# A four-layer network on one core: the mixer stage as one run over both batch pairs, and conditioning units that scan backward over the forward scan's result

## The chip, the cores and the metric

The kernel runs on one core of one Trainium2 chip. Its time is the device time of that core in microseconds (us), here the median of three runs. A core has TensorE for matrix products (PE; its weight loads are listed as PEld), VectorE (DVE), ScalarE (ACT), GpSimd (POOL), and SyncE (SP), which issues the DMAs. PE, DVE, ACT and POOL each take their instructions in a fixed order and wait for each other on semaphores.

## The reference

Four batches of 256 tokens by 256 channels pass through four layers. Ahead of each layer stands a conditioning step, and `x = x + layer(condition(x, f, f, w, u, emb))`, where `f` is the same side input each time:

```python
tf = sigmoid(sum(time_emb, -1))[:, None, None]
decay = exp(-exp(w))[None, :] * (0.5 + 0.5 * tf[:, :, 0])
ek = exp(minimum(k, 30)); ekv = ek * v                 # k = v = f
nf, df = scan(a * decay + ekv, b * decay + ek)         # over 256 tokens, forward
nb, db = the same, reverse=True
euk = exp(minimum(u + k, 30))
num = nf + nb - ekv + euk * v
den = df + db - ek + euk
out = sigmoid(r) * (num / maximum(den, 1e-8)) * (0.8 + 0.2 * tf)   # r = x
```

The layers are a Mamba2 mixer (32 heads of 64, state 128, conv of 4 taps, SiLU gate, RMS norm, output projection), a mixture of 16 experts (4 picked) with a shared one, latent attention with 16 heads, and grouped-query attention with a mixture of 8 experts.

## The kernel before, in words

Channels lie on the 128 partitions. The four batches are two **pairs**; one pair is 2 batches x 256 tokens = 512 columns (`TOK`), and a tensor of 256 channels by one pair is 1024 columns (`UNIT`). The stages follow one another with a barrier of all engines between them: `stage_condition`, `stage_mixer`, `stage_moe` (first mixture), `stage_latent_attention`, `stage_gqa`, `stage_moe` (second).

A **conditioning unit** (`CondUnit`) makes the factor `m` = num / den x scale of one conditioning step for one pair. It depends on `f` alone, not on `x`, so the kernel makes the units of later layers beside the matrix work of earlier stages. `CondUnit.vector` returns a list of 26 small steps for DVE: `add_u` (2), four scans (`den`, `den_b`, `num`, `num_b`; 2 steps each, and each step is two scans of 256 columns), `combine` (2, adds the backward denominator), `add_own` (2), `bound` (2), `invert` (8 reciprocals of 128 columns) and `factor` (2). `take(steps, n)` issues the next n of them. POOL makes the numerator in four operations on 1024 columns (`pool_numerator`), and ACT makes one exponential (`scalar`). `stage_condition` makes both pairs' units for the mixer, one after the other, and `make_h(pair)` ends each: `h = (tanh(x/2) + 1) * m`. `stage_mixer` carries the two units of the first mixture, the first mixture those of latent attention, and latent attention those of the last layer.

**The mixer** goes over the pairs (`for i in range(PAIRS)`), and for each pair over 16 tiles of 128 inner channels, two heads a tile, in `STEPS = 16 + 4` steps. At step s each engine works on several tiles at once:

- PE: `x_like(s+2)` and `gate_like(s)` project (4 matmul instructions of 512 columns each, since float32 goes in two passes), `spread_cum` (two per step) writes each head's running decay sums to PSUM, `turn_x(s-1)` transposes, `project_out(s-4)` projects out, `mix(s-3)` multiplies values with decays (16 instructions, one head on output partitions 0 to 63, then the other on 64 to 127).
- ACT: `begin_conv`, `exp_decay` (two per step, 4 exponentials each), `tanh_conv`, `tanh_gate`, `square_g`.
- POOL: `scale_decay` twice (128x768) and `add_square` once (128x512), and at four steps one operation of `pool_numerator`.
- DVE: `taps` (3 instructions of the convolution, read from PSUM), `gated(s-3)` (y and g), `silu_x`, `take_x(s-1)`, `silu_gate(s)`, and then `take(cond, 2)`, two steps of the unit. That last place in a step is called the **slot** below.

Before its first tile each pair has a **prologue**: the projections for dt, B and C, the softplus (`softplus_cum`), the running sums and their split in three bfloat16 parts (`cum_parts`), their transposes (`turn_cum`, `row_cols`), and the products of B and C (`key_query`, taken by DVE as `scores`). B and C go through the same PSUM bank, convolution and SiLU as the tiles. After its last tile each pair has an **end**: the sum of squares over channels (one matmul), its inverse root on ACT (a logarithm and an exponential), and `add_to_x`. Semaphore counts set the order; nothing is scheduled by a planner.

The memory of the prologue is shared: `z`, `soft`, `dt` and `cum` lie in the buffer of `gate`, and `root` in that of `y`, so that a pair's prologue has to wait for the pair before. PSUM has eight banks, all in use.

Of the kernel before, what the change touches and what calls it, by code (L numbers as in the profile page):

```python
# [91 lines left out]
class Net:  # L92


    def __init__(self, nc, stack, dram):
# [23 lines left out]
        self.dcol = sb("dcol", [P, 4 * KT * BATCH])  # L119
        self.scol = sb("scol", [P, BATCH])  # L120
# [44 lines left out]
class CondUnit:  # L165


    VECTOR_LINKS = 7 * KT

    def __init__(self, net, c, sems):  # L170
        self.net, self.c = net, c
        (self.u_ready, self.euk_ready, self.scans_done, self.own_ready,
         self.factor_made, self.num_steps) = sems

    def pool_numerator(self, pair, turn):

        net, nc = self.net, self.net.nc
        pool = nc.gpsimd
        both = slice(pair * UNIT, (pair + 1) * UNIT)

        def own():
            pool.wait_ge(self.euk_ready, turn + 1)
            pool.tensor_tensor(net.euk[:], net.euk[:], net.e[:, both], ALU.subtract) \  # L183
                .then_inc(self.own_ready, 1)

        def own_times_f():
            pool.wait_ge(self.own_ready, turn + 1)
            pool.wait_ge(self.num_steps, 3 * turn)
            pool.tensor_tensor(net.own_f[:], net.euk[:], net.f[:, both], ALU.mult) \
                .then_inc(self.num_steps, 1)  # L190

        def add_backward():
            pool.wait_ge(self.scans_done, turn + 1)
            pool.tensor_tensor(net.num[:], net.num[:], net.num_b[:], ALU.add) \
                .then_inc(self.num_steps, 1)

        def add_own():
            pool.wait_ge(self.num_steps, 3 * turn + 2)
            pool.tensor_tensor(net.num[:], net.num[:], net.own_f[:], ALU.add) \
                .then_inc(self.num_steps, 1)  # L200

        return own, own_times_f, add_backward, add_own
# [7 lines left out]
    def vector(self, link, pair, turn):  # L210
# [4 lines left out]

        def columns(k):
# [5 lines left out]
        done = [None] * KT  # L222

        def on(k, op):
            done[k] = link.mark(op)

        def after(k):
            if done[k] is not None:
                v.wait_ge(*done[k])
# [9 lines left out]
        def scan(out, x, reverse=False):  # L239
            order = slice(None, None, -1) if reverse else slice(None)  # L240

# [33 lines left out]
        def invert(part):  # L275
# [4 lines left out]
            if part == INVERT_PARTS - 1:  # L280
                link(op)
# [157 lines left out]

# [1855 lines left out]
```

## Time and profile before

| | |
|---|---|
| median of 3 runs | 1437.3 us (1430.36 to 1439.8) |
| the profiled execution | 1430.53 us, its span 1428.7 us |
| granted TensorE clock, mean | 0.952 of full speed |
| conditioning stage | 0 to 62.5 us |
| mixer stage | 62.5 to 459.4 us |
| first mixture | 459.4 to 739.5 us |
| latent attention | 739.5 to 939.5 us |

The stage bounds are read from the timeline (the first instruction of a stage after the barrier). A busy share is the time in which an engine has an instruction under way. That time includes waits inside an instruction, for example for a port of the memory. The time ahead of an instruction in which its engine stood idle stands in square brackets at the end of its row, with the instruction that ended the wait.

### The profile page before, as it was taken

The page shows a single profiled execution, that of the slowest core. Times are in us where ns is not written, and L with a number is a line of the kernel's source. Part 1 is how long each engine was busy: PE and PEld are TensorE (multiplying, and loading weights), DVE is VectorE, ACT ScalarE, POOL GpSimd, SP SyncE. Part 2 cuts the span into 40 slices and gives each one's busy share as a digit, 9 for nine tenths or more (in the row PEclk, how much of TensorE's full clock was granted, in tenths as well). Part 3 has the DMA queues.
Part 4 walks back from the last instruction along what each step waited for, and adds up shares of the span by engine and source line. Part 5 has one row for each costly group of instructions (what it writes and reads, how often), then busy time and mean ns, then how long its engine had stood idle before and what let it go on. Part 6 is the DMA issues. An engine that isn't in the chain of part 4 may idle for free. (4 is left out here: it accounts for less than half of the span.)

```text
span 1428.7 us, 14494 instructions
## 1 busy us (share of the span) xinstructions
PE 1208.1 (85%) x4614; PEld 642.9 (45%) x4614; DVE 863.4 (60%) x1306; ACT 585.7 (41%) x1732; POOL 512.9 (36%) x499
## 2 busy tenths in 40 slices
PE   0277998688996899999987998978799887987998
PEld 0033454243443444444444655633585346834443
DVE  8789986699993563265236839639750596414222
ACT  1154554354544222222225545647572585700110
POOL 5634576045754110020002827627551375500000
PEclk9999999999998799999997999989899998997999
DMA  6000000000021300000020000030000000000000
GB/s 256 22 1 1 1 1 1 1 0 1 1 83 70 129 1 0 1 0 0 34 111 37 1 0 1 2 140 0 1 2 0 0 1 1 2 0 8 0 0 30
DMA packets 4730, 33.53 MB, mean 23 GB/s; under 512 B 528, under 2 KB 912, under 8 KB 2768
## 3 DMA queue, kind: packets, MB, share of 16 engines
q1 hardware_dynamic: 4656, 32.61, 5.8%
q8 instruction: 38, 0.62, 0.2%
q14 instruction: 36, 0.29, 0.1%
HBM read 31.56 MB, written 1.05 MB: 23 GB/s over the span
## 5 line engine op out<-in xcount | busy, mean ns | idle before, releaser
L780 POOL TENSOR_TENSOR decays<-decays,scores 128x768 f32<-128x768 f32 x64 | 123.3, 1929 | 173.9 <-ACT decays L716 173.6
L1371 POOL TENSOR_TENSOR prob_latent<-prob_latent,inverse_latent 128x128 f32<-128x128 f32 (+1 forms) x128 | 78.6, 637 | 187.1 <-DVE inverse_latent L1361 186.9
L1962 POOL TENSOR_TENSOR euk<-m,weights 128x256 f32<-128x256 f32 x80 | 91.1, 1157 | 91.3 <-DVE m L1983 79.7
L542 PE MATMUL pg<-h,weights 128*128 128x512 f32 (+1 forms) x136 | 66.3, 610 | 65.2 <-PEq L328 62.7
L1067 PE MATMUL ph<-h,weights 128*128 128x512 f32 x256 | 116.8, 601 | 0.0
L542 PE MATMUL px<-h,weights 128*128 128x512 f32 x136 | 73.2, 664 | 32.9 <-DVE conv L852 32.8
L716 ACT ACTIVATE decays<-pcum,neg_cum 128x256 f32<-128x256 f32 (+1 forms) x256 | 87.9, 450 | 12.4 <-PE pcum L595 12.4
L1211 DVE TENSOR_TENSOR mid<-up,ph 128x512 f32<-128x512 f32 x44 | 30.2, 686 | 96.8 <-ACT up L1124 96.8
L1124 ACT ACTIVATE up<-ph 128x512 f32<-128x512 f32 x44 | 26.3, 597 | 140.1 <-PE ph L1067 140.1
L1371 POOL TENSOR_TENSOR prob_gqa<-prob_gqa,inverse_gqa 128x128 f32<-128x128 f32 (+1 forms) x128 | 62.2, 508 | 57.8 <-DVE inverse_gqa L1361 56.1
L852 DVE SCALAR_TENSOR_TENSOR conv<-px,pp,conv 128x510 f32<-128x510 f32 (+2 forms) x102 | 75.2, 737 | 11.8 <-ACT conv L681 9.3
L688 ACT ACTIVATE tanh_x<-conv 128x512 f32<-128x512 f32 x36 | 22.5, 630 | 144.0 <-DVE conv L852 144.0
L1067 PEld LDWEIGHTS ph<-h,weights 128*128 128x128 f32 x256 | 49.4, 193 | 62.2 <-issue 62.1
L183 POOL TENSOR_TENSOR euk<-euk,e 128x1024 f32<-128x1024 f32 x8 | 21.2, 2652 | 150.8 <-ACT euk L208 150.8
L622 PE MATMUL py<-decays,x_tok 128*64 128x128 f32 (+1 forms) x512 | 71.2, 332 | 0.0
L636 PE MATMUL pout<-g,weights 128*128 128x512 f32 x128 | 64.0, 624 | 6.3 <-DVE g L908 6.3
L622 PEld LDWEIGHTS py<-decays,x_tok 128*64 128x64 f32 x512 | 51.9, 137 | 36.1 <-issue 24.5
L1238 DVE TENSOR_TENSOR mid<-act_out,ph 128x512 f32<-128x512 f32 x22 | 15.1, 688 | 81.4 <-ACT act_out L1118 81.4
L1118 ACT ACTIVATE act_out<-ph 128x512 f32<-128x512 f32 x26 | 15.5, 597 | 112.9 <-PE ph L1067 112.8
L542 PEld LDWEIGHTS pg<-h,weights 128*128 128x128 f32 (+1 forms) x136 | 23.4, 191 | 85.0 <-issue 84.6
L1085 PE MATMUL pmoe<-hidden,weights 128*128 128x512 f32 x128 | 60.2, 591 | 0.0
L1067 PE MATMUL ph<-h,moe_rest 128*128 128x512 f32 x128 | 57.5, 592 | 0.0
(317 smaller groups left out, 2955.7 us busy)
## 6 DMA issues: line engine op xcount, KB each, us to landing
weights<-in_w_mixer SPq DMA_DIRECT2D x2, 2048.0 KB, 18.2
weights<-in_w_moe SPq DMA_DIRECT2D x2, 1536.0 KB, 7.7
moe_rest<-in_w_moe SPq DMA_DIRECT2D x2, 1536.0 KB, 13.5
weights<-in_w_gqa SPq DMA_DIRECT2D x1, 3072.0 KB, 9.6
weights<-in_w_gqa SPq DMA_DIRECT2D x1, 2048.0 KB, 14.1
weights<-in_w_moe SPq DMA_DIRECT2D x1, 1920.0 KB, 8.6
weights<-in_w_mixer SPq DMA_DIRECT2D x1, 1536.0 KB, 12.5
weights<-in_w_moe SPq DMA_DIRECT2D x1, 1152.0 KB, 11.9
```

The source lines that it names most:

```text
L542: op = nc.tensor.matmul(out[0:m, :], w[:, col + k * m:col + (k + 1) * m], net.h[:, ds(i * PAIR + k * TOK, TOK)], start=(k == 0), stop=(k = ...
L622: op = nc.tensor.matmul(py[rows, b * SEQ + r * P:(b + 1) * SEQ], x_tok[:, s % 3, b * ST + r, rows], decays[:, head % 4, b, cols], start=(r ...
L636: op = nc.tensor.matmul(pout[k][:], w[:, at:at + P], g[:, s % 2, :], start=(s == 0), stop=(s == N - 1))
L716: op = nc.scalar.activation(decays[:, head % 4, b, r * SEQ:r * SEQ + n], pcum[r][:, b * n:(b + 1) * n], ACT.Exp, bias=neg_cum[:, at:at + 1])
L780: nc.gpsimd.tensor_tensor(decays[:, head % 4], decays[:, head % 4], scores[:], ALU.mult).then_inc(decay_scaled, 1)
L852: op = v.scalar_tensor_tensor(out, src, conv_w(n, TAPS - 1 - k), out, ALU.mult, ALU.add)
L1067: op = nc.tensor.matmul(out[:], wt[:, n * D + k * P:n * D + (k + 1) * P], net.h[:, ds(i * PAIR + k * TOK, TOK)], start=(k == 0), stop=(k = ...
L1085: op = nc.tensor.matmul(pout[k][:], wt[:, 2 * D + k * P:2 * D + (k + 1) * P], hidden[:, m % 2, :], start=(m == 0), stop=(m == N - 1))
L1124: nc.scalar.activation(up[:, m % 2, :], ph1[m % 2][:], ACT.Copy) \
L1211: v.tensor_tensor(mid[:, m % 2, :], up[:, m % 2, :], ph3[m % 2][:], ALU.mult) \
L1371: op = nc.gpsimd.tensor_tensor(self.prob[:, slot, cols], self.prob[:, slot, cols], self.inverse[:, slot, t:t + 1].to_broadcast([P, P * (t ...
L1962: op = nc.gpsimd.tensor_tensor(out[:, :, s, :], src[:, :, 1 - s, :], sin[:, None, s, :].to_broadcast([P, 4, HALF]), ALU.mult)
```

## The change

Three things change together.

1. **Unit algebra.** The forward scan writes `den_b` (or `num_b`), and the backward scan runs over that result, not over the input, with an initial value that `edge` computes from the forward scan's last column (`edge_scale` = decay / (1 - decay squared)). Multiplied by `ccol` = 1 - decay squared, its result is the sum of forward and backward less the token's own term. So `combine` goes, `add_own` multiplies by `ccol` and adds in one instruction of 256 columns (four for the denominator, and four for the numerator, which was POOL's), and POOL keeps one operation of four (`own_f = euk * f`). A unit now has 28 steps. This holds in every stage that carries a unit.
2. **Conditioning stage.** It makes pair 0's unit alone. Pair 1's unit and `make_h(1)` go into the slots of the mixer. Five small DVE instructions that make `ccol` and `edge_scale` come in.
3. **Mixer.** One loop over 32 tiles of both pairs (`T` from 0 to 36). Pair 1's prologue is spread over steps 11 to 15, and pair 0's end falls on step 20. `z`, `cum`, `dt`, `root` and `scaled` get buffers of their own, and `scores`, `parts`, `neg_cum` and `dt_tok` hold both pairs. The slots take 3 steps of a unit (T even, or under 6) or 2, until the 85 steps of three units and `make_h(1)` are used up in step 32. `mix` alternates the two heads. The norm weights are folded into the output weights by ACT (`fold_norm`, in steps 0 to 2), not by POOL. `sel` shrinks to one column per head that is broadcast.

```diff
 class CondUnit:
...
-        def own():
...
-        def own_times_f():
...
-        def add_backward():
...
-        def add_own():
...
+        nc.gpsimd.wait_ge(self.euk_ready, turn + 1)
+        nc.gpsimd.wait_ge(self.factor_made, turn)
+        nc.gpsimd.tensor_tensor(net.own_f[:], net.euk[:], net.f[:, pair * UNIT:(pair + 1) * UNIT],
+                                ALU.mult).then_inc(self.own_ready, 1)
...
+        def edge(name, f):
...
+        def backward(name, out, f):
             def step(k):
                 here, _ = columns(k)
+                after((name, "edge"))
+                for b in range(BB):
+                    seq = slice(b * SEQ, (b + 1) * SEQ)
+                    at = ((name == "num") * KT + k) * BB + b
+                    op = v.tensor_tensor_scan(out[:, here][:, seq][:, ::-1],
+                                              column(net.dcol, k, b).to_broadcast([P, SEQ]),
+                                              f[:, here][:, seq][:, ::-1],
+                                              net.edge[:, at:at + 1], ALU.mult, ALU.add)
+                on((name, k), op)
...
+        def add_own(name, out, own):
...
+                    op = v.scalar_tensor_tensor(out[:, here][:, seq], out[:, here][:, seq],
+                                                column(net.ccol, k, b), own[:, here][:, seq],
+                                                ALU.mult, ALU.add)
...
         stages = [
-            add_u,
-            scan(net.den, net.e), scan(net.den_b, net.e, True),
-            scan(net.num, net.ev), scan(net.num_b, net.ev, True),
-            combine(net.den, net.den_b), add_own, bound,
+            add_u, forward("den", net.den_b, net.e), edge("den", net.den_b),
+            backward("den", net.den, net.den_b),
+            forward("num", net.num_b, net.ev), edge("num", net.num_b),
+            backward("num", net.num, net.num_b),
+            add_own("den", net.den, net.euk), bound, add_own("num", net.num, net.own_f),
         ]
...
 def stage_condition(net):
...
-                take(steps[pair], scans)
-                dve.wait_ge(ev_ready, pair + 1)
-                take(steps[pair], len(steps[pair]))
-                make_h(pair)
+            dve.wait_ge(e0_exp, 1)
+            take(steps, 2 * KT + 1)
+            dve.wait_ge(ev_ready, 1)
+            take(steps, len(steps))
+            make_h(0)
...
+DT_STEP, B_STEP, C_STEP, CUM_STEP, TURN_STEP, QUERY_STEP = 11, 12, 13, 12, 13, 15
...
-            def mix(i, s):
...
+            def mix(T):
...
+                for b in range(BB):
+                    for r in range(ST):
+                        cols = slice(0, SEQ) if r == 0 else slice(SEQ, TRI)
+                        for hh in range(TILE_HEADS):
...
+            for T in range(STEPS + 1):
+                if T < TILES:
+                    x_like(T)
+                if T == 1:
+                    turn_cum(0)
+                    key_query(0)
+                if T == DT_STEP:
+                    gate_like((1, "dt"))
+                if T == TURN_STEP:
+                    turn_cum(1)
+                if T == QUERY_STEP:
+                    key_query(1)
...
         def _(act):
...
+                if T == DT_STEP:
+                    softplus(1)
+                if 0 <= T - LAG_HEADS < TILES:
+                    exp_decay(2 * (T - LAG_HEADS))
+                if T < TILES:
+                    tanh_conv(T)
+                    tanh_gate(T)
+                if 0 <= T - LAG_HEADS < TILES:
+                    exp_decay(2 * (T - LAG_HEADS) + 1)
...
+                for i in range(PAIRS):
+                    if T == (i + 1) * N + LAG_OUT:
+                        make_root(i)
...
         def _(dve):
...
+            for T in range(STEPS + 1):
+                if T < TILES:
+                    taps(T)
...
+                if T == DT_STEP:
+                    softplus_in(1)
+                if T == CUM_STEP:
+                    cum_parts(1)
+                if T == TURN_STEP:
+                    row_cols(1)
+                if T == QUERY_STEP:
+                    take_scores(1)
+                if 0 <= T - LAG_Y < TILES:
+                    gated(T - LAG_Y)
...
+                for i in range(PAIRS):
+                    if T == (i + 1) * N + LAG_OUT:
+                        add_to_x(i)
+                take(cond, 3 if T % 2 == 0 or T < 6 else 2)
```

The order moves at three places that matter below. PE in step 15 of the changed kernel, from its first projection to its last product (`pcum<-bc` is `key_query(1)`, `pcum<-parts,sel` is `spread_cum`, `py<-` is `mix(12)`):

```order
L603 MATMUL px<-h,weights 128x512 x2
L648 MATMUL pcum<-bc 128x256
L650 MATMUL pcum<-bc 128x128
L648 MATMUL pcum<-bc 128x256
L650 MATMUL pcum<-bc 128x128
L663 MATMUL pcum<-parts,sel 128x512
...
L674 MATMUL pt<-ident,xs 128x128 x4
L707 MATMUL pout<-g,weights 128x512 x2
L692 MATMUL py<-decays,x_tok 64x256 x2
L692 MATMUL py<-decays,x_tok 64x128 x2
```

Before, these products of B and C stood in a pair's second step, ahead of which no `mix` was due. Now six groups of a full step, `mix` among them, are queued behind them, and `spread_cum` writes the banks that DVE has yet to empty. The two heads' matmuls now alternate (one row, x2), where before each head's four stood together.

ACT at the start of step 11 of the changed kernel, the softplus of pair 1 (`cum<-cum`) between the convolution's start and the next decays:

```order
L766 ACTIVATE conv<-px,pp 128x512
L778 ACTIVATE cum<-cum 32x512
L780 ACT_TABLE_LOAD
L780 ACTIVATE cum<-cum 32x512
L805 ACT_TABLE_LOAD
L805 ACTIVATE decays<-pcum,neg_cum 128x256 x2
L805 ACTIVATE decays<-pcum,neg_cum 128x128 x2
L773 ACTIVATE tanh_x<-conv 128x512
```

Before, the softplus stood ahead of a pair's first step, with no decays behind it. Now two loads of ACT's function tables and the softplus stand ahead of the decays and of `tanh_x`.

DVE in steps 22 and 23 of the changed kernel, the end of one step, its slot, and the next (`gate<-` is `silu_gate(22)`, `conv<-` is `taps(23)`):

```order
L976 SCALAR_TENSOR_TENSOR gate<-tanh_g,gate 128x512
L221 TENSOR_SCALAR euk<-f,pp 128x512
L232 SCALAR_TENSOR_TENSOR den_b<-dcol,e 128x256 x4
L960 SCALAR_TENSOR_TENSOR conv<-px,pp,conv 128x2x255
L960 SCALAR_TENSOR_TENSOR conv<-px,pp,conv 128x2x254
L960 SCALAR_TENSOR_TENSOR conv<-px,pp,conv 128x2x253
L1012 SCALAR_TENSOR_TENSOR y<-xs,pp,py 128x512
```

The same place before holds one group of two steps:

```order
L867 SCALAR_TENSOR_TENSOR gate<-tanh_g,gate 128x512
L247 SCALAR_TENSOR_TENSOR num<-dcol,ev 128x256 x4
L852 SCALAR_TENSOR_TENSOR conv<-px,pp,conv 128x2x255
L852 SCALAR_TENSOR_TENSOR conv<-px,pp,conv 128x2x254
L852 SCALAR_TENSOR_TENSOR conv<-px,pp,conv 128x2x253
L901 SCALAR_TENSOR_TENSOR y<-xs,pp,py 128x512
```

The slot grew from two steps of a unit to two or three, and slots now stand in steps 0 to 32 of one run, where before they stood in steps 2 to 14 of each pair.

## Rows read from the trace of the kernel before

**Rows 1.** The page: busy time, share of the span and instructions.

```profile
PE 1208.1 (85%) x4614; PEld 642.9 (45%) x4614; DVE 863.4 (60%) x1306; ACT 585.7 (41%) x1732; POOL 512.9 (36%) x499
```

**Rows 2.** Windows: stretch, length, busy us (instructions) of each engine, granted clock, DMA.

```profile
35.60:62.50 26.90, 0.00 (x0) 0.00 (x0) 26.54 (x35) 1.06 (x2) 12.85 (x4) 1.00 0.00 0
62.50:94.30 31.80, 22.27 (x58) 9.42 (x59) 21.46 (x36) 12.29 (x19) 14.45 (x16) 0.95 0.10 25
94.30:231.60 137.30, 124.03 (x528) 62.44 (x526) 128.32 (x140) 69.98 (x172) 80.21 (x42) 0.98 0.00 1
231.60:289.30 57.70, 40.94 (x143) 19.41 (x144) 32.03 (x52) 24.44 (x48) 15.19 (x10) 0.91 0.00 0
426.50:459.40 32.90, 21.26 (x86) 10.51 (x86) 10.92 (x17) 14.96 (x32) 15.19 (x10) 0.90 0.17 72
739.50:939.50 200.00, 174.86 (x936) 106.10 (x936) 128.29 (x249) 104.95 (x356) 97.29 (x136) 0.93 0.07 27
```

**Rows 3.** Timeline of the conditioning stage, DVE: start, length, what, wait ahead.

```profile
8.25 1.27 DVE L396 TENSOR_SCALAR e<-f 128x1024 f32<-128x1024 f32 x1 [2.00 <-DMA f<-in_f]
9.44 6.70 DVE L247 TENSOR_TENSOR_SCAN den<-dcol,e 128x256 f32<-128x256 f32 x4
20.71 2.41 DVE L247 TENSOR_TENSOR_SCAN num_b<-dcol,ev 128x256 f32<-128x256 f32 x4
```

**Rows 4.** Timeline of DVE in the mixer, two slots and the step between them.

```profile
118.42 6.42 DVE L247 TENSOR_TENSOR_SCAN den_b<-dcol,e 128x256 f32<-128x256 f32 x4
124.77 2.28 DVE L852 SCALAR_TENSOR_TENSOR conv<-px,pp,conv 128x510 f32<-128x510 f32 x3
...
129.54 0.68 DVE L867 SCALAR_TENSOR_TENSOR gate<-tanh_g,gate 128x512 f32<-128x512 f32 x1
130.14 8.75 DVE L247 TENSOR_TENSOR_SCAN num<-dcol,ev 128x256 f32<-128x256 f32 x4
138.81 1.50 DVE L852 SCALAR_TENSOR_TENSOR conv<-px,pp,conv 128x510 f32<-128x510 f32 x2
```

**Rows 5.** Timeline of POOL in the second of these slots.

```profile
130.00 1.89 POOL L780 TENSOR_TENSOR decays<-decays,scores 128x768 f32<-128x768 f32 x1 [6.29 <-ACT decays L716]
131.86 1.65 POOL L792 TENSOR_TENSOR square_sum<-square_sum,square 128x512 f32<-128x512 f32 x1
133.47 2.73 POOL L183 TENSOR_TENSOR euk<-euk,e 128x1024 f32<-128x1024 f32 x1
136.16 2.18 POOL L780 TENSOR_TENSOR decays<-decays,scores 128x768 f32<-128x768 f32 x1
```

**Rows 6.** Timeline of DVE: a slot of reciprocals, the next y, the slot of `factor`.

```profile
216.01 1.75 DVE L279 RECIPROCAL den<-den 128x128 f32<-128x128 f32 x2
...
220.88 0.75 DVE L901 SCALAR_TENSOR_TENSOR y<-xs,pp,py 128x512 f32<-128x512 f32 x1 [0.77 <-PE py L622]
...
225.36 3.97 DVE L289 SCALAR_TENSOR_TENSOR m<-num,scol,den 128x512 f32<-128x512 f32 x2
```

**Rows 7.** Timeline of PE and ACT: one `mix`, one projection, one head's decays.

```profile
191.20 2.22 PE L622 MATMUL py<-decays,x_tok 128*64 128x256 f32 x16
...
193.35 1.98 PE L542 MATMUL px<-h,weights 128*128 128x512 f32 x4
...
194.04 1.36 ACT L716 ACTIVATE decays<-pcum,neg_cum 128x256 f32<-128x256 f32 x4
```

**Rows 8.** Timeline of the prologue: a table load, the first and last of `cum_parts`.

```profile
74.89 1.28 ACT L688 ACT_TABLE_LOAD   x1
...
80.67 0.67 DVE L831 SCALAR_TENSOR_TENSOR gate<-gate 32x512 f32<-32x512 f32 x1
...
85.93 0.42 DVE L844 CAST parts<-y 32x512 bf16<-32x512 f32 x1
```

**Rows 9.** Windows at pair 0's end; the third figure from the right is the clock.

```profile
230.80:234.10 3.30, 0.00 (x0) 0.00 (x0) 3.23 (x6) 2.40 (x6) 0.00 (x0) 1.00 0.00 0
235.00:241.70 6.70, 5.79 (x14) 2.74 (x14) 0.00 (x0) 3.19 (x10) 6.70 (x5) 0.50 0.00 0
```

More of the change, by code:

```diff
@@ L214, in vector, with column @@
         v = nc.vector
+        def column(table, k, b):
+            at = (c * KT + k) * BATCH + pair * BB + b
+            return table[:, at:at + 1]
         def columns(k):
@@ L237, in add_u, with forward @@
                 op.then_inc(self.u_ready, 1)
-        def scan(out, x, reverse=False):
-            order = slice(None, None, -1) if reverse else slice(None)
+        def forward(name, out, x):
             def step(k):
@@ L349, in _ @@
                                         ALU.mult).then_inc(ev_ready, 1)
-                for step in unit.pool_numerator(pair, pair):
-                    step()
+                if pair == 0:
+                    unit.pool(0, 0)
         @block.scalar
@@ L391, in _ @@
                 ALU.mult).then_inc(cols_ready, 1)
[L392 removed]
+            dve.wait_ge(cols_ready, 3)
+            link(v.tensor_scalar(net.ccol[:], net.dcol[:], -1.0, 1.0, ALU.mult, ALU.add))
+            link(v.scalar_tensor_tensor(net.ccol[:], net.dcol[:], 1.0, net.ccol[:], ALU.add,
+                                        ALU.mult))
+            link(v.tensor_scalar(net.ccol[:], net.ccol[:], 1e-10, None, ALU.max))
+            link(v.reciprocal(net.edge_scale[:], net.ccol[:]))
+            link(v.tensor_tensor(net.edge_scale[:], net.edge_scale[:], net.dcol[:], ALU.mult))
+            steps = unit.vector(link, 0, 0)
             for pair in range(PAIRS):
@@ L811, in _ @@
             v = nc.vector
+            _, make_h, _ = net.mixer_input
+            link = Links(dve, links)
             half_d = net.pp[:, PP_D:PP_D + N]
@@ new lines, in add_to_x @@
+                    out = net.x[:, i * PAIR + k * TOK:i * PAIR + (k + 1) * TOK]
+                    v.tensor_tensor(scaled[:], pout[k][:], root[:], ALU.mult) \
+                        .then_inc(out_free, 1)
+                    dve.wait_ge(out_free, KT * i + k + 1)
+                    link(v.tensor_tensor(out, out, scaled[:], ALU.add))
+            cond = []
+            for turn, (unit, pair) in units.items():
+                cond += unit.vector(link, pair, turn)
+                if turn == 1:
+                    cond.append(partial(make_h, 1))
@@ L952 @@
+            assert not cond
 class Experts:
@@ L1143, in _ @@
                 for i in range(PAIRS):
-                    for step in unit.pool_numerator(i, i + turn0):
-                        step()
+                    unit.pool(i, i + turn0)
         @block.vector
```

672 lines of the change are left out of this document (361 added, 311 removed).

## The prediction

> **What bounds the kernel now.** The page first: PE is busy 85% of the span, DVE 60% [rows 1]. That mean hides stages with different limits, so the windows come next [rows 2]. In the conditioning stage's second half (26.9 us for pair 1's unit) PE does nothing and DVE is busy throughout. In the mixer's full steps (94.3 to 231.6, steps 2 to 15 of pair 0; pair 1's stretch differs by 0.1 us) DVE is busy 128.3 of 137.3 us and PE 124.0. At the joint of the pairs (231.6 to 289.3) DVE works 32.0 of 57.7 us, and at the mixer's end 10.9 of 32.9. So the mixer is bound by DVE with PE close behind, and its joint and ends are chains.
>
> Then the timeline of DVE, because its busy time is not all work. A full step without its slot is 5.4 us (124.77 to 130.14), and four scans undisturbed take 2.4 us [rows 3, 4]. In the slots they take 6.4 and 8.75 us [rows 4]. POOL's rows tell why: its operations and the four scans alternate, each scan ending as the POOL operation under way ends [rows 5]. So a burst of POOL per step (decays, squares, decays) holds up a slot with three or more instructions that contend by 6.42 - 2.35 = 4.1 us, one with two by 3.97 - 1.4 = 2.6, and a burst with a unit's operation in it by 8.75 - 2.35 = 6.4. Reciprocals are not held up (1.75 for two) [rows 6]. The Trainium skill ("SBUF — State Buffer", "Who interferes with whom") says that a DVE instruction with two inputs in SBUF and a GpSimd one that reads SBUF block each other whole; by that rule, which the alternation agrees with, the new scans and add_own contend as the old ones did.
>
> I keep the account of the mixer in DVE's time: before, 397 us = 321 busy + 76 idle. The busy part is 21.5 + 128.3 + 32.0 + 128.2 + 10.9 [rows 2]. Of it some 75 us are blocking: 29.4 per unit, in nine slots of 1.6 to 6.4 (the 4.1, 6.4 and 2.6 above are three of them), and 16 on the gates.
>
> **The change, part by part.**
>
> *Conditioning stage.* The second half goes: -26.9 [rows 2]. Five small instructions come ahead of e(0), chained; I take 0.25 us each, +1.2 (the path through ev, e(1) and the scans moves whole, since e(1) now meets ev; bounds 0, if the wait for f at 8.25 [rows 3] hides it, and 2). add_own for two tensors against combine and add_own for one, two edges and their links: +1.1. Pair 1's ev moves up beside the scans, in place of the POOL operation that blocked them there (9.44, 6.70 for four [rows 3]): 0. Sum: -24.6, the mixer starts at 37.9. Its weights are not late: DMA moves nothing more in 35.6 to 62.5 [rows 2].
>
> *Mixer, DVE's work.* The third unit adds 22.1: scans 9.4, add_u 0.9, reciprocals 6.6, factor 1.4, bound 0.7, eight add_own at 0.34 (2.7), two edges 0.4. The other two units change by +1.1 each: four operations of 512 columns (2.4) go, 2.7 + 0.4 and links come. make_h(1) adds 1.2. Blocking: I went through the slots of steps 2 to 32. Eleven hold three or more contending instructions beside a full burst (11 x 4.2 = 46), three have POOL's own_f in it (16), five hold two (13), those of steps 11, 15 and 20 come late, behind most of the burst (5), and the gates keep 5: 85, against 75 before. Bounds: 60, if the gates and slots fall between bursts, 100 if every slot pays. Busy time: 321 + 22 + 2 + 1 + 10 = 356.
>
> *Mixer, idle time.* The ramp keeps 10 of its 31.8 - 21.5. The joint's 25.7 goes. The full steps lose 18 now; in eight slots of reciprocals PE stays the bound: I keep 9. The last end had 22: 4 less, because step 31's slot holds reciprocals, so taps(31) isn't late and PE doesn't sit as it did at 230.8 to 234.1, 2.7 less if the clock then doesn't halve [rows 9], 2.6 less for three shorter mixes, and 1.3 more, because a table load of 1.28 us [rows 8] now stands between logarithm and exponential: 14. Into the stream come four new waits of DVE for PE, since PE's order is written for a prologue without a mix:
> - Step 11: softplus_in 1.4, Exp and Ln 1.3, two table loads 2.56, then exp_decay 1.36, and only then PE's second spread_cum (0.7), turn_x, project_out (1.8) and mix (1.4): y(8) comes 10.8 us after taps(11), 9.3 late.
> - Step 13: PE's product for C waits for taps(13), then C 1.8, turn_x 0.4, out 1.8, mix 1.4: 5.5, of which 5.0 wait.
> - Step 15: spread_cum waits for take_scores(1). Then 0.7 + 1.8 + 0.7 + 0.4 + 1.8 + 1.4 = 6.8 of waiting.
> - Step 20: turn_x(19) and mix(17) wait for the logarithm behind exp_decay and a table load: 3.1 + 1.3 + 0.7 + 0.5 + 1.4 = 7.0.
> The durations are those of [rows 7, 8]. Sum 28, bounds 15 and 40. Idle time: 10 + 9 + 28 + 14 = 61. cum_parts (80.67 to 86.35, 5.7 us [rows 8]) stays at two, in work that is counted.
>
> The mixer takes 356 + 61 = 417 us and ends at 455, against 459.4: **-4.4**. A count step by step (12.3 us for step 3, 20 to 22 for steps 11, 12 and 13, 8.4 to 12.4 for most) came to 418.
>
> *The mix.* Heads on separate halves of the output alternate. Now 16 instructions take 2.22 us, and the next projection begins 2.15 after [rows 7]. 3072 columns at the pace of a projection (4 x 512 in some 1.8) would be 2.6, so the heads overlap only where one follows the other. I take 1.3, in the sum already. Bounds: 1.3 and 2.15. If nothing overlaps, the four waits, three mixes at the end and the steps that PE bounds lose 0.87 each: +11. The Trainium skill ("TensorEngine Tiling (Array Packing)", "Key Properties") lets column tiles run matmuls in parallel; that rule gives the 1.3, and the trace agrees as far as its 0.4 us of overlap goes.
>
> *What moves to ACT.* fold_norm, 16 operations, about 0.35 us each (a decay of like size takes 1.36 / 4 [rows 7]), in steps 0 to 2, behind which ACT waited for DVE; POOL had them in the ramp and no one waited: 0. The work that hides them is DVE's own first slots (2.1 and 2.6 us); without it, +4.
>
> *Other stages.* In the first mixture PE is the bound and unit work is beside it: 0. Latent attention: POOL loses three operations of about 2.5 us per pair out of its 97 us, DVE gains 1.1 per unit [rows 2]. Each such operation stretches a head by about 1 us: -3 (bounds -6 and +2). The second half of the kernel is untouched.
>
> **Sum:** -4.4 - 3 = -7 on a profiled execution of 1430.5, so 1423.5. That execution was the fastest of those shown; the median is 6.8 higher, and I carry that over: **1430**.
>
> **The rivals.**
> - *Faster than forecast: slots and waits overlap.* If bursts slide out of the longer slots (blocking 60 for 85) and the four waits are filled because PE works ahead (15 for 28), the mixer takes 25 + 13 less: 1430 - 30 = 1400. For it: reciprocal slots pay nothing [rows 6], and the joint's 25.7 us are gone for sure. Against: POOL's burst starts 3 us after each taps, exactly at the slot, by ACT's order, which stays.
> - *Slower: the clock halves in the new waits.* After 3.3 us without a matmul the granted clock fell to 0.50 (1.2 GHz) for 6.7 us, and PE's work there took double [rows 9]. In steps 11 to 15 and 20 PE sits for longer, and it is on the path right behind. Five us of work that takes double at each of four places is +20, and blocking above the forecast's, at 90, +5: 1430 + 25 = 1455. It decides if the waits are 28 and not 15: then a fall behind each is enough. Against: in full steps such a fall was hidden by DVE.
> - *The mix doesn't overlap*, the change doing less than it says there: 1430 + 11 = 1441.
> - *DVE's added work is cheaper than its cover*: included in the first.
>
> **How the numbers follow.** A measurement of this kernel can tell about 1% (14 us) from no change. Chances: forecast 0.46, faster rival 0.31, slower 0.14, no overlap 0.09. The likeliest is 1430, by itself 1418 to 1443. The range that leaves out 2 in 10: 1394 to 1450. Faster by over 1% (under 1423): the faster rival and the forecast's low end, 0.37. Slower by over 1% (above 1452): 0.13. Within: 0.50.
>
> **What the changed profile would show.** First projection at about 38 us; the mixer's end (the next stage's tanh) at 455. DVE busy about 356 in the mixer. mix 1.3 us for 16 instructions, y at the end spaced 0.9 closer. Slots with scans at 6.6 and more, with own_f 9 to 10. Waits of DVE for y of 9, 5, 7 and 7 us in steps 11, 13, 15 and 20. A latent stage of 197 us. The prediction is wrong if slots are much shorter than POOL's burst, if the four waits are missing, or if the granted clock stands at 0.5 for long between 180 and 300 us.

## The result, and the profile after

The changed kernel takes 1445.7 us (median of 9 runs, 1443.6 to 1448.3) for 1436.7 of the kernel before (9 runs): ratio 1.0063, 95% interval 1.0043 to 1.0084. It is 9 us slower where 7 us faster were forecast. The profiled execution took 1443.8 us, its span 1441.9 for 1428.7, so 13.2 us more. A program on this chip has a slower state: a run over 1.5% above its kernel's fastest is left out of every ratio below.

The page and the windows by stage, in the order of [rows 1, 2]: conditioning, mixer, first mixture, latent attention, the stage behind it. The last three figures are the granted clock, DMA's share and GB/s.

```profile
PE 1200.5 (83%) x4614; PEld 629.0 (44%) x4614; DVE 880.5 (61%) x1359; ACT 595.4 (41%) x1751; POOL 430.8 (30%) x459
...
0.70:38.90 38.20, 0.00 (x0) 0.00 (x0) 33.81 (x52) 6.86 (x9) 7.99 (x4) 1.00 0.59 239
38.90:479.50 440.60, 327.64 (x1340) 151.13 (x1340) 360.01 (x434) 203.11 (x461) 175.86 (x99) 0.89 0.03 10
479.50:758.40 278.90, 267.38 (x660) 121.75 (x660) 124.51 (x208) 67.16 (x102) 5.89 (x5) 0.97 0.07 25
758.40:954.30 195.90, 173.77 (x936) 105.43 (x936) 130.13 (x261) 103.63 (x354) 83.39 (x130) 0.95 0.07 28
954.30:1299.90 345.60, 302.68 (x1352) 190.87 (x1353) 188.42 (x322) 200.01 (x801) 156.34 (x214) 0.95 0.04 15
```

The mixer's window before, up to the first instruction behind its barrier (459.7; the 459.4 given above is 0.3 early):

```profile
62.50:459.70 397.20, 331.86 (x1340) 163.84 (x1340) 320.94 (x381) 191.54 (x441) 205.26 (x120) 0.96 0.04 14
```

The mixer starts at 38.9 (37.9 forecast) and ends at 479.5 (455 forecast). It takes 440.6 us for 397.2 before: 43.4 more, against 23.6 saved ahead of it and 3.1 in latent attention (195.9 for 199.0, since that stage ended at 938.5 before, not at 939.5). In the account of the prediction DVE is busy 360.0 us in it, for 321 before and 356 forecast, and idle 80.6, for 76 before and 61 forecast. The joint's 25.7 us of idle time are gone, and yet DVE's idle time has not fallen. The clock's mean there is 0.89 for 0.96: 0.11 x 2 x 441, some 97 us, at the lower of its two levels (1.2 GHz), for some 32 before.

The conditioning stage, DVE's timeline, to be read beside [rows 3]:

```profile
4.75 0.18 DVE L404 TENSOR_SCALAR ccol<-dcol 128x32 f32<-128x32 f32 x1
...
6.03 0.69 DVE L414 TENSOR_SCALAR e<-f 128x1024 f32<-128x1024 f32 x1
...
10.70 6.69 DVE L232 TENSOR_TENSOR_SCAN den_b<-dcol,e 128x256 f32<-128x256 f32 x4
...
17.62 2.68 DVE L257 TENSOR_TENSOR_SCAN den<-dcol,edge,den_b 128x256 f32<-128x256 f32 x4
20.22 2.41 DVE L232 TENSOR_TENSOR_SCAN num_b<-dcol,ev 128x256 f32<-128x256 f32 x4
...
25.46 1.65 DVE L271 SCALAR_TENSOR_TENSOR den<-den,ccol,euk 128x256 f32<-128x256 f32 x4
```

The five small instructions take 1.28 us in all (1.2 forecast). The first scans take 6.69 under POOL's operation as before (6.70). Two prices were too low: four scans that start from `edge` take 2.68 us, not 2.41, and an `add_own` 0.41, not 0.34. That is 1.1 us a unit.

Where DVE waited in the mixer (the brackets at the rows' ends: us waited, releaser), in steps 11, 13, 15, 20 and twice in 21:

```profile
183.57 0.75 DVE L1012 SCALAR_TENSOR_TENSOR y<-xs,pp,py 128x512 f32<-128x512 f32 x1 [9.37 <-PE py L692]
...
221.87 0.75 DVE L1012 SCALAR_TENSOR_TENSOR y<-xs,pp,py 128x512 f32<-128x512 f32 x1 [6.92 <-PE py L692]
...
257.84 0.75 DVE L1012 SCALAR_TENSOR_TENSOR y<-xs,pp,py 128x512 f32<-128x512 f32 x1 [7.81 <-PE py L692]
...
314.70 0.75 DVE L1012 SCALAR_TENSOR_TENSOR y<-xs,pp,py 128x512 f32<-128x512 f32 x1 [8.64 <-PE py L692]
...
326.82 2.31 DVE L960 SCALAR_TENSOR_TENSOR conv<-px,pp,conv 128x510 f32<-128x510 f32 x3 [3.48 <-ACT conv L766]
...
332.45 0.75 DVE L1012 SCALAR_TENSOR_TENSOR y<-xs,pp,py 128x512 f32<-128x512 f32 x1 [3.32 <-PE py L692]
```

And what PE itself waited for between 160 and 330 us (us in total, times, longest), from the view of waits:

```profile
PE px L603 <- DVE conv L960: 21.9, 7, 5.6
PE pt L674 <- ACT root L827: 8.2, 1, 8.2
PE pcum L663 <- DVE scores L990: 7.6, 1, 7.6
PE pout L707 <- DVE scaled L1027: 5.5, 1, 5.5
PE pcum L663 <- ACT decays L805: 4.6, 4, 3.2
PE pg L603 <- DVE h L442: 3.3, 1, 3.3
```

Both lists together are the chains: DVE waits for y, and PE, which owes it, has stood for DVE or ACT just before. The fourth line is one that the prediction lacks. The timeline of PE and ACT at the joint shows it:

```profile
308.96 1.28 ACT L827 ACT_TABLE_LOAD   x1
...
310.25 0.69 ACT L827 ACTIVATE root<-pt,pp 128x512 f32<-128x512 f32 x1
...
311.09 1.09 PE L674 MATMUL pt<-ident,xs 128*128 128x128 f32 x4 [8.20 <-ACT root L827]
...
320.17 3.75 PE L707 MATMUL pout<-g,weights 128*128 128x512 f32 x4 [5.52 <-DVE scaled L1027]
...
323.72 2.25 PE L603 MATMUL px<-h,weights 128*128 128x512 f32 x4
```

`turn_x(19)` and `mix(17)` stand behind the root's logarithm, as forecast. Then `project_out(16)` may not write `pout` until `add_to_x(0)` has read it, and `x_like(21)` stands behind it on PE, so taps(21) and y(18) are late too.

`mix` and the projection behind it, beside [rows 7]: 1.52 us and a start 1.45 later, for 2.22 and 2.15.

```profile
182.00 1.52 PE L692 MATMUL py<-decays,x_tok 128*64 128x256 f32 x16
...
183.45 1.98 PE L603 MATMUL px<-h,weights 128*128 128x512 f32 x4
```

A slot of step 2 beside POOL's burst, to be read as [rows 4, 5]: the scans last as long as the burst.

```profile
79.17 2.90 DVE L257 TENSOR_TENSOR_SCAN den<-dcol,edge,den_b 128x256 f32<-128x256 f32 x2
...
79.62 1.90 POOL L879 TENSOR_TENSOR decays<-decays,scores 128x768 f32<-128x768 f32 x1 [2.24 <-ACT decays L805]
81.49 2.72 POOL L186 TENSOR_TENSOR own_f<-euk,f 128x1024 f32<-128x1024 f32 x1
81.99 6.08 DVE L232 TENSOR_TENSOR_SCAN num_b<-dcol,ev 128x256 f32<-128x256 f32 x4
84.18 2.19 POOL L879 TENSOR_TENSOR decays<-decays,scores 128x768 f32<-128x768 f32 x1
```

### The profile page after: what moved, and what is told of

Read it like the earlier page. It is cut to its first block and busy times, and to the rows that moved or that the text cites. A ratio compares the mean times of both kernels' runs of the same rounds, so it can differ in the third digit from the quotient of the medians.

```text
span 1441.9 us, 14560 instructions
## 1 busy us (share of the span) xinstructions
PE 1200.5 (83%) x4614; PEld 629.0 (44%) x4614; DVE 880.5 (61%) x1359; ACT 595.4 (41%) x1751; POOL 430.8 (30%) x459
## 5 line engine op out<-in xcount | busy, mean ns | idle before, releaser
L603 PE MATMUL px<-h,weights 128*128 128x512 f32 x140 | 84.6, 734 | 56.5 <-DVE conv L960 56.4
L603 PE MATMUL pg<-h,weights 128*128 128x512 f32 (+1 forms) x136 | 71.4, 651 | 42.5 <-PEq L339 39.2
L186 POOL TENSOR_TENSOR own_f<-euk,f 128x1024 f32<-128x1024 f32 x8 | 20.4, 2548 | 160.3 <-ACT euk L193 160.3
L603 PEld LDWEIGHTS px<-h,weights 128*128 128x128 f32 x140 | 28.2, 223 | 88.9 <-DVE conv L960 63.2
L663 PE MATMUL pcum<-parts,sel 96*128 96x512 bf16 (+1 forms) x128 | 44.6, 357 | 24.2 <-ACT decays L805 16.6
L1012 DVE SCALAR_TENSOR_TENSOR y<-xs,pp,py 128x512 f32<-128x512 f32 x32 | 23.8, 743 | 54.7 <-PE py L692 54.7
## 6 DMA issues: line engine op xcount, KB each, us to landing
moe_rest<-in_w_moe SPq DMA_DIRECT2D x2, 1536.0 KB, 13.2
```

The lines of the kernel that those rows point to most:

```text
L603: op = nc.tensor.matmul(out[0:m, :], w[:, col + k * m:col + (k + 1) * m], net.h[:, i * PAIR + k * TOK:i * PAIR + (k + 1) * TOK], start=(k ...
L663: nc.tensor.matmul(out, sel[:, h:h + 1].to_broadcast([3 * HEADS, P]), rows, start=True, stop=False)
```

## The experiments

Every ratio is to the kernel before on the same chip. The changed kernel's own ratio is 1.0063, and "against the changed kernel" is the quotient of the two, worked out here, times 1446. Theory A: the order of instructions on the queues makes chains, which ate the joint's gain. Theory B: the halved clock did it. Theory C: the third unit's work and blocking on DVE did it.

**The waits gone.** The same work in another order at five places, and one copy of `pout` (two instructions on ACT). The edit in outline:

```diff
 ACT  step 11:  - softplus(1); exp_decay; tanh_conv; tanh_gate; exp_decay
                + exp_decay; tanh_conv; tanh_gate; exp_decay; square_g; softplus(1)
 PE   12, 13:   - x_like((1, b or c)); turn_x; project_out; mix
                + turn_x; project_out; mix; x_like((1, b or c))
 PE   14, 15:   key_query(1) behind mix of step 14, not at the head of 15
 DVE  14, 15:   take_scores(1) behind silu_gate(14), not behind taps(15)
 PE   20:       - sum_squares(0); turn_x; mix; project_out
                + turn_x; mix; project_out; sum_squares(0)
 ACT  20:       + activation(scaled[:, k], pout[k], Copy) for both k, behind begin_conv(20)
 DVE:           add_to_x(0) in step 21, from the copy
```

> The changed kernel with its order at five places rewritten, the same work otherwise: softplus(1) on ACT behind both decays of step 11; the products for pair 1's B and C on PE behind the mix of their step; key_query(1) and take_scores(1) a step earlier; pair 0's sum of squares behind the mix of step 20, with pout copied out by ACT so that project_out(16) doesn't wait for add_to_x(0), which comes a step later. Theory A (the order makes the loss): in the changed kernel's trace DVE waits 9.4, 8.3, 7.8, 8.6 and 6.8 us in steps 11, 13, 15, 20 and 21, 41 us in all; with the waits gone some 10 of it comes back as PE's own time, so the mixer takes 410 us for 440.6 and the kernel 1415 (1408 to 1422). Theory B (the clock makes the loss, since PE has too little work there and is granted 1.2 GHz whatever the order): the clock row stays as it is, and the gain is at most 12: 1434. Theory C (the third unit's work and its blocking on DVE make the loss): DVE is busy 360 us already, the steps get full and no more than 10 us come back.

1419.7 us, ratio 0.9902 (0.9883 to 0.9921): 23 us off the changed kernel. That is A's number (1408 to 1422), at its slow end, and twice what B and C allow. The mixer's window:

```profile
38.80:456.30 417.50, 320.53 (x1340) 147.95 (x1340) 358.62 (x434) 204.15 (x463) 175.71 (x99) 0.91 0.03 11
```

DVE's busy time is what it was (358.6), and its idle time 59 for 81. The clock's mean rose only from 0.89 to 0.91, so most of the time came from order and not from the clock. Of the 30 us expected back 23 came: steps 11, 13, 15 and 21 still wait 5.8, 4.0, 2.9 and 5.5.

**The clock kept up**, first try. Matmuls into a free PSUM bank, read by nobody:

```diff
+            def keep_busy(bank, n):
+                for _ in range(n):
+                    nc.tensor.matmul(bank[:], net.ident[:], net.h[:, 0:TOK], start=True, stop=True)
```

> The changed kernel with 74 more matmuls of 512 columns, whose results nobody reads, at the six places where PE waits 3 to 8 us between 175 and 320 us (steps 11, 12, 13, 14, 15, 20): PE keeps its activity, and no order or wait changes. Theory A: the waits are chains over ACT, DVE and PE, in which PE's part is small; the time stays within 5 us of the changed kernel's 1445, or gets a little worse where a filler runs over. Theory B: the granted clock stands at 1.0 from 175 to 325 us, where it was 0.5 for 48 us, and the time falls by 15 or more, to 1430 or below.

1470 us (the median of the four runs that count), ratio 1.0253 (1.0228 to 1.0278). The fillers were mis-sized: each came out as two instructions 0.45 us apart, so they were longer than the waits and made chains of their own. It tells nothing of the theories.

**The clock kept up, half the filler.**

> As the run with the clock kept, at the same six places, with 33 idle matmuls for 74: each of them turned out to take 0.91 us (two passes), so that the fillers were twice as long as the waits that they stood in and made them longer. Now they take 2.7 to 6.4 us, somewhat less than the wait at each place. Theory A (chains): PE is at full clock at these places, and the time stays within 5 us of the changed kernel's 1445. Theory B (the halved clock costs some 15 to 20 us in these chains): 1430 or below. The waits of steps 13 and 15, where PE's projections and spreads stand on the path at 1.2 GHz, tell most: 6.9 and 7.8 us now, 5.0 and 6.0 if the clock holds.

1441.8 us, ratio 1.0063 (1.0040 to 1.0087), the changed kernel's own. The windows of steps 11 to 20 and of the mixer's end, first the changed kernel's, then this run's, show where the clock (third figure from the right) was held up and where it wasn't:

```profile
175.00:325.00 150.00, 103.89 (x420) 49.55 (x419) 110.92 (x140) 63.78 (x141) 53.98 (x31) 0.85 0.00 1
425.00:479.50 54.50, 36.73 (x166) 17.46 (x166) 35.25 (x42) 26.99 (x59) 26.31 (x16) 0.89 0.20 80
```

```profile
175.00:321.00 146.00, 124.99 (x492) 58.43 (x491) 111.04 (x141) 64.10 (x143) 53.96 (x31) 0.96 0.00 1
421.00:476.60 55.60, 38.28 (x166) 17.41 (x164) 33.70 (x40) 25.98 (x58) 26.31 (x16) 0.84 0.20 79
```

Its timeline of DVE in steps 13, 15 and 20:

```profile
220.22 0.75 DVE L1034 SCALAR_TENSOR_TENSOR y<-xs,pp,py 128x512 f32<-128x512 f32 x1 [5.36 <-PE py L696]
...
254.46 0.75 DVE L1034 SCALAR_TENSOR_TENSOR y<-xs,pp,py 128x512 f32<-128x512 f32 x1 [6.38 <-PE py L696]
...
310.93 0.75 DVE L1034 SCALAR_TENSOR_TENSOR y<-xs,pp,py 128x512 f32<-128x512 f32 x1 [8.25 <-PE py L696]
```

The waits are 5.4, 6.4 and 8.3 for 6.9, 7.8 and 8.6, 3.4 us less, and the taps of step 21 wait 1.4 for 3.5. Step 11 waits 9.4 as before. Some of it comes back at the end, where the clock is lower than in the changed kernel: the last four waits for y add up to 16.4 us for 12.9. The mixer got 2.4 shorter, and the median nothing that can be measured. Theory B wanted 15 us or more from these places and is out as the main cause. That the clock costs 3 us or so there is not excluded, as the interval is that wide. Outside these places the clock was left as it was, and no run tried it there.

**Small units**, in the changed kernel and in the one before: each instruction of the mixer's units on 16 of 512 columns.

```diff
-                    seq = slice(b * SEQ, (b + 1) * SEQ)
+                    seq = slice(b * w, (b + 1) * w)      # w = 8 in the mixer's units
```

> The changed kernel with the three units of the mixer done on 16 of each 512 columns (every instruction, wait and the two factors stay; the rest of each unit's work is left out): the loop of the mixer by itself. Theory A: steps fall to PE's 9.1 us, the waits stay: 35 to step 2, 30 x 9.1, 30 of waits, 24 at the end, so the mixer takes 362 and is no shorter than that of the kernel before with small units. Theory C: the waits hide under nothing else and are small, the mixer takes 340 or less, 20 under the kernel before with small units. The kernel: 1362 by A, 1340 by C.

> The kernel before with the two units of its mixer done on 16 of each 512 columns (the rest of their work is left out). The full steps fall to PE's 9.1 us, 18.5 us less a pair: the mixer takes 360 us for 397 and the kernel 1400. Theory A wants the mixer of the changed kernel with small units at or above this, theory C 20 us below.

Ratios 0.9779 (0.9758 to 0.9800) and 0.9877 (0.9855 to 0.9899). The windows of the two mixers, first the changed one's:

```profile
38.00:437.00 399.00, 317.06 (x1340) 146.74 (x1340) 297.29 (x434) 200.48 (x462) 162.85 (x99) 0.93 0.03 12
```

```profile
73.50:450.60 377.10, 328.55 (x1340) 164.19 (x1340) 283.95 (x381) 190.90 (x442) 183.47 (x120) 0.97 0.04 14
```

Both are longer than expected (362 and 360). I had the steps fall to PE's pace, but POOL's bursts still hold DVE up, and it stays busy 297 and 284 us. In the kernel before the blocking moved to the gates (`gated`, `silu_x` and `silu_gate` took 110 us for 82). In the changed one the short instructions of the units took it over (76 us, where their shortest times add up to some 22). The changed loop with little unit work is 22 us longer than the old one, which has the joint. That speaks for A, but not cleanly: 13 of the 22 are busy time and only 9 idle time. Three units cost 41.6 us here (440.6 - 399.0), two cost 20.0 before.

**mix by heads**, the loops `for hh` outermost as before.

> The changed kernel with the 16 matmuls of mix in the order of the kernel before, head by head. The prediction's term: 0.87 us at each of 13 places, 11 us slower, 1456. The changed trace shows the next projection 1.45 us behind mix's start, for 2.15 before, so 0.7 a place: 9 slower, 1454. If mix is off the path nearly everywhere: within 3 of 1445.

1449.9 us, ratio 1.0124 (1.0095 to 1.0152): 9 us slower than the changed kernel, as the term said (11, or 9 by the measured 0.7).

**The unit outside.** Pair 1's first unit goes back to the conditioning stage.

```diff
-        UNIT_START = {1: 0, 2: 11, 3: 22}
+        UNIT_START = {2: 0, 3: 14}
-                take(cond, 3 if T % 2 == 0 or T < 6 else 2)
+                take(cond, 2)
```

> The changed kernel with pair 1's first unit back in the conditioning stage (the new scans and add_own there too), and the mixer's two units from steps 0 and 14 at two steps of a unit each. The stage gets some 25 us longer. Theory A (order and waits make the loss, a unit among steps bounded by PE or by waits costs about 14 us, as the runs with small units say: 42 for three): the mixer gets 14 to 20 us shorter and the kernel 5 to 10 slower, 1453. Theory C (the third unit costs its work and its blocking, 49 us of DVE's time): the mixer gets 45 to 49 us shorter and the kernel 20 faster, 1425.

1449.4 us, ratio 1.0115 (1.0089 to 1.0141): 7.5 us slower, A's number. The mixer's window:

```profile
65.10:485.90 420.80, 325.10 (x1340) 150.13 (x1340) 320.28 (x393) 202.36 (x461) 173.16 (x98) 0.90 0.03 11
```

DVE is busy 40 us less, and the mixer is only 20 shorter: the rest turns into idle time, which is 100 here. This is also the cleanest comparison with the kernel before, as both mixers carry two units. DVE is busy 320.3 us here and 320.9 there, and the mixer is 23.6 longer, all of it idle time. The unit inside is a gain, though a small one, and theory C is out as the cause of the loss.

**The kernel before with mix alternated.**

> The kernel before with one part of the change alone: mix with its heads alternated, so that PE waits for both decays before the first matmul. The last three mixes of each pair stand on the path there: 0.6 to 0.9 us each, six in all, so 4 to 5 us faster: 1432 by medians for 1436. In the full steps DVE is the bound, and nothing changes. If the wait for the second decay costs what the overlap gives, no change.

1434.0 us, ratio 1.0007 (0.9984 to 1.0031): nothing, where 4 to 5 us were expected. The window of its mixer tells where they went, beside the sum of [rows 2] (321 busy, 76 idle):

```profile
66.50:464.30 397.80, 316.37 (x1340) 144.72 (x1340) 326.72 (x381) 192.16 (x441) 205.76 (x120) 0.95 0.04 14
```

DVE's idle time is 5 us less (71), and its busy time 5.8 more in the same instructions. That the work meets POOL's bursts more often is how I read it; no run tried it, and these are two single executions.

**Small bursts.** `scale_decay` on 16 of each 384 columns (the rest of the scaling is left out).

> The changed kernel with POOL's scaling of the decays done on 16 of each 384 columns (the rest of the scaling is left out): POOL's burst of 2 x 1.9 us a step nearly goes, squares and own_f stay. The prediction's blocking term was 85 us (80 in the slots, 5 on the gates); by the trace it is 67 and 17. If those are really DVE held up by POOL, DVE is busy 65 to 75 us less in the mixer, of which PE's 9 to 10 us a step and the waits give back half: the mixer 400 for 440, the kernel 1405. If the long scans are long for another reason: within 10 of 1445.

1398.9 us, ratio 0.9754 (0.9711 to 0.9797). The mixer's window:

```profile
38.20:436.00 397.80, 319.29 (x1340) 149.64 (x1340) 297.10 (x434) 203.02 (x461) 73.18 (x99) 0.91 0.03 12
```

DVE is busy 63 us less with its own instructions unchanged (65 to 75 expected), and the mixer is 43 shorter. Blocking by POOL's bursts is real, and of about the forecast's size (the squares and `own_f` stay). The Trainium skill ("SBUF — State Buffer", "Who interferes with whom") has a DVE instruction with two SBUF inputs and a GpSimd one that reads SBUF block each other whole; these 63 us agree with it.

**The joint freed.** Only steps 20 and 21 of the changed kernel are altered.

```diff
+        SUM_AT = [25, TILES + LAG_OUT]      # sum_squares, make_root
+        square_sum has a half for each pair; pout copied by ACT as above (into net.h, pair 0)
-                    if T == (i + 1) * N + LAG_OUT:
+                    if T == SUM_AT[i] + 1 - i:
                         add_to_x(i)
```

> The changed kernel with only the joint of the pairs freed: pair 0's pout is copied out by ACT at step 20 (into pair 0's h, which nobody reads any more), its squares have a sum of their own, and sum, root and add_to_x(0) move to steps 25 and 26; steps 11 to 15 stay. Theory A (orders of instructions): the waits of 8.6 us in step 20 and 3.5 + 3.3 in step 21 go, of which the last two stood in no term of the prediction (PE's project_out(16) waits for DVE's add_to_x(0), and x_like(21) behind it); two copies on ACT are beside other work: 12 to 15 us off, ratio to the kernel before 0.997. If the root's two table loads (2.6 us) and its logarithm in step 25 hold up decays there: 8 off. Theory C (DVE's work and blocking): no more than 4 off.

1440.5 us, ratio 1.0045 (1.0025 to 1.0064): 3 us off, not 12. Its timeline in step 25:

```profile
369.80 0.69 ACT L828 ACTIVATE root<-pt,pp 128x512 f32<-128x512 f32 x1
...
370.63 1.09 PE L675 MATMUL pt<-ident,xs 128*128 128x128 f32 x4 [13.60 <-ACT root L828]
...
375.89 0.75 DVE L1017 SCALAR_TENSOR_TENSOR y<-xs,pp,py 128x512 f32<-128x512 f32 x1 [10.28 <-PE py L693]
```

Steps 20 and 21 went from 36.1 to 19.7 us, and the chain came up again where the root now stands: behind `tanh_conv`, so behind DVE's taps, with `turn_x` and `mix` behind it.

**The joint freed, root ahead of tanh_conv.**

```diff
                     exp_decay(2 * (T - LAG_HEADS))
+                if T in SUM_AT:
+                    make_root(SUM_AT.index(T))
                 if T < TILES:
                     tanh_conv(T)
```

> The run with the joint freed, with ACT's make_root ahead of tanh_conv in its step, where ACT has idle time, and not behind it. By theory A the 10 us wait of step 25 was the same chain as in step 20 (turn_x and mix behind a logarithm that stands behind work that needs taps): it shrinks to 2 or less, and the joint's whole price shows: 12 to 14 us off the changed kernel, ratio 0.997. If sum and root cost the step 8 us wherever they stand: ratio 1.004 as before.

1432.9 us, ratio 0.9979 (0.9965 to 0.9994): 12 us off the changed kernel. One place on ACT's queue is worth 9 us, with the same instructions. The wait of step 25 is gone (0.2 us for 10.3). The mixer's window:

```profile
38.90:467.80 428.90, 324.73 (x1340) 149.17 (x1340) 362.49 (x434) 204.03 (x463) 177.40 (x99) 0.90 0.03 11
```

**Orders rewritten further**, and two runs behind it.

> The run with the waits gone, and what its trace left: (1, dt)'s product at the end of PE's step 11 and softplus_in behind DVE's slot, since PE stood 3 us for make_h(1) and the gate waited for softplus_in behind taps(11) (a wait of 5.8 us); x_like of steps 13 and 14 behind the first spread and the gate (4.0 us); and the joint as in the run with the joint freed, sum and root in step 25 (5.5 us). Theory A: 10 of these 15 us come back, the mixer takes 407 and the kernel 1409 by medians of the chip before, ratio 0.983. If steps are now bounded by PE and by DVE's blocking: ratio 0.988 to 0.990, as before these edits.

1433.6 us, ratio 0.9992 (0.9972 to 1.0011): a miss, and worse than the first order. Step 25 waited 11.8 us for the reason just given (root stood behind `tanh_conv` here too). The wait for y in step 11 was gone, but taps(12) waited 3.3 us in its place.

> The run with the waits gone (its steps 11 to 15 as they were), with pair 0's sum, root and add_to_x in steps 25 and 26 and root ahead of tanh_conv. Theory A: the 5.5 us of waiting left in step 21 go, and the 6 us of table loads and root beside them: 5 to 6 us off, ratio 0.986. If step 25 takes them over: 0.990.

> As the run before, with three unit steps for two in slots 7 and 9, so that make_h(1) stands in slot 9 and no longer right ahead of step 11, whose product for (1, dt) needs it. If step 11's wait (5.8 us) comes from h (PE stands 3 us, and its clock halves after it): 3 to 4 us off, ratio 0.983. If it comes from the gate's product behind softplus_in: no change.

```diff
-                take(cond, 3 if T % 2 == 0 or T < 6 else 2)
+                take(cond, {7: 3, 9: 3, 10: 1}.get(T, 3 if T % 2 == 0 or T < 6 else 2))
```

1420.0 us, ratio 0.9889 (0.9870 to 0.9908), and 1420.7, ratio 0.9895 (0.9876 to 0.9914). Neither can be told from the 0.9902 of the run with the waits gone. Freeing the joint further did take away the 5.5 us of step 21, but the last four waits for y came to 17.4 us for 12.8, at a mean clock of 0.84 for 0.89; why, is open. Earlier h doesn't help either. The timeline of step 11 in the last shows why:

```profile
170.37 2.30 DVE L965 SCALAR_TENSOR_TENSOR conv<-px,pp,conv 128x510 f32<-128x510 f32 x3
172.58 0.73 DVE L935 TENSOR_SCALAR z<-pg,pp 32x512 f32<-32x512 f32 x1
...
173.37 2.67 PE L604 MATMUL pg<-h,weights 128*128 128x512 f32 x4 [3.53 <-DVE z L935]
...
181.23 0.75 DVE L1017 SCALAR_TENSOR_TENSOR y<-xs,pp,py 128x512 f32<-128x512 f32 x1 [7.20 <-PE py L693]
```

PE's gate product waits for `softplus_in`, which reads the bank `pg` behind taps(11); with that chain h is not what is late. (The wait for y was 5.9 us in the run before and is 7.2 here.)

## Why the prediction was wrong, step by step

**Right.** The conditioning stage: -23.6 for -24.6, and the missing 1.0 is the two prices above. Latent attention: -3.1 for -3. DVE's busy time: 360 for 356. The excess over 356 is what scans from `edge` and `add_own` cost more in three units (3 us). The mix: 1.45 for 1.3, and +9 without it for 11. In the mixer's idle time the ramp (9.2 for 10) and step 11 (9.4 for 9.3). fold_norm at no cost in the ramp fits the row, but no run tried it alone.

**Right by luck.** Blocking came to some 84 us for 85, but from two errors that cancel: 67 in the slots for 80 (their spans less the undisturbed times), and 17 on gates and other instructions for 5. The gates had 16 before and kept them.

**Wrong: the step "Into the stream come four new waits of DVE for PE ... Sum 28, bounds 15 and 40", and with it "Idle time: 10 + 9 + 28 + 14 = 61".** It was 80.6, and these 20 us are most of the mixer's 24:

- Steps 12 and 13: 8.9 for 5.0, with taps((1, b)) and `bc` waiting 0.7 each beside y; step 15: 7.8 for 6.8; step 20: 8.6 for 7.0. With the clock held up 3.4 of these 6.5 went (the run with half the filler).
- Step 21: 6.8, where the sum has no term. That is the error of kind: I followed what stands behind the root on ACT and PE, and not who needs `pout` next. In the kernel before this wait stood inside the joint, which I had struck out whole. With these 6.8 the forecast would have been no change. With the clock held up 2.1 of them went.
- The last steps: 18.2 for 14. Step 31's y was 3.3 late, where I had struck out the wait of [rows 9].
- Steps bounded by PE, and gaps under 0.4 us: 11.6 for 9.

The end is 1445.7 for 1430: +24 in the mixer, +1 ahead of it, -4 behind it (latent attention as forecast; 3.5 in other stages, of which 1.6 stands in the last stage, which carries no unit), and -5 because the changed kernel's profiled execution lay 1.9 below its median, where I had carried over 6.8.

That last step, "the median is 6.8 higher, and I carry that over", was wrong too, and it hid a part of what the change gains. The conditioning stage of the kernel before takes 62.5 us in its own trace, but 66.5 and 73.5 us in the traces of the two runs that leave that stage as it was (mix alternated, small units). The difference starts where POOL's `num<-num,num_b` and DVE's two `den<-den,den_b` begin within 0.2 us of each other. In the first trace POOL takes 5.18 us and DVE 1.26, in the second POOL 2.70 and DVE 3.40:

```profile
49.82 1.26 DVE L263 TENSOR_TENSOR den<-den,den_b 128x512 f32<-128x512 f32 x2
```

```profile
49.48 3.40 DVE L263 TENSOR_TENSOR den<-den,den_b 128x512 f32<-128x512 f32 x2
```

So the forecast stands on an execution with a short conditioning stage. The change takes both operations away, and its mixer starts between 38.0 and 38.9 us in the traces of all runs that keep its conditioning stage. That fits the spread of the nine runs of each kernel, 12.5 us before and 4.6 after. How often each case comes up in the kernel before is not shown.

**The rivals.** The slower one (1455) comes nearest in time and had the wrong mechanism: the clock did stand at 1.2 GHz for some 97 us of the mixer (mean 0.89), 45 of them between 175 and 325 us, which was one of the signs of being wrong. Held up at the places of the waits it gave back nothing that the median shows, where the rival has 20 us. The faster one (blocking 60, waits 15) is out on both counts. Its price was added up wrongly besides: its terms, 25 and 13, make 38 and so 1392, where the prediction takes 30 off and has 1400. That mix doesn't overlap is out.

**What stays open.** The orders tried leave some 15 us of these waits in steps 11 to 21 of the best kernel, of the change's 41.5, and I know the chain of step 11 alone. Why the last steps wait longer when earlier waits go is not known. Nor is it shown whether another place of the slots could avoid POOL's bursts.

## What to carry to other kernels

A joint of two halves that is merged away leaves its chains behind: for each resource that the old joint waited for (a PSUM bank, a table, a shared sum) find its next writer and what is queued behind that writer, and put the long link where the engines behind it have slack. Here nearly the same instructions in a better order (two copies came in) turned a ratio of 1.0063 into 0.9889. Time that DVE gains while POOL works in bursts is not free time: price the slot by the burst, and try first to shrink the burst.

## What the runs showed that I had not expected

- Holding the granted clock up between 175 and 321 us (mean 0.96 for 0.85) shortened four waits by 0.4 to 2.1 us each and changed the ratio not at all: the halved clock was a mark of the waits more than their cause.
- With mix alternated in the kernel before, the execution that was traced had 5 us less idle time of DVE and 5.8 more busy time in the same instructions.
- With the units' columns cut to a thirtieth, DVE's busy time fell by 37 us of 321 and 63 of 360 only, less than their rows lost (107 to 36 us before, 144 to 76 after). In the kernel before the gates took over the blocking, and in the changed one the units' short instructions kept it.
